# Gate and up products of a 4-bit-format feed-forward in three passes, and its rounding spread over two engines

## What is computed

```python
x = x + 0.5 * _L0_ffn_ref(_layernorm(x), w_gate, w_up, w_down)
x = x + _L0_attn_ref(_layernorm(x), L0_attn_W, L0_attn_b)
x = x + 0.5 * _L0_ffn_ref(_layernorm(x), w_gate, w_up, w_down)
x = x + 0.5 * _L1_ffn_ref(...)   # mixture of experts
x = x + _L1_attn_ref(...)        # causal attention
x = x + 0.5 * _L1_ffn_ref(...)
...
def fp4_quant_dequant(x):        # blocks of 16 along the last dim
    scale = max(max(abs(xb)) / 6.0, 1e-12)
    xn = xb / scale
    idx = searchsorted(_MID, abs(xn))        # grid 0, 0.5, 1, 1.5, 2, 3, 4, 6
    return _GRID[idx] * sign(xn) * scale
def fp4_linear(x, w):
    return einsum('bsk,nk->bsn', fp4_quant_dequant(x), fp4_quant_dequant(w))
gate, y = fp4_linear(x, w_gate), fp4_linear(x, w_up)     # 256 -> 704
h = silu(gate) * y
return fp4_linear(h, w_down)                              # 704 -> 256
```

## Time and profile before

| | us |
|---|---|
| median of three runs | 2346.11 (2342.72 to 2347.78) |
| span of the profiled execution | 2324.6 |
| first feed-forward, first to last L523 | 68.17 to 361.06 |
| second feed-forward, first to last L523 | 473.99 to 770.69 |
| TensorE busy in the span | 1960.7 (84%) |
| VectorE busy | 1764.5 (76%) |
| ScalarE busy | 958.9 (41%) |
| GpSimd busy | 907.5 (39%) |

### The profile page before, as it was taken

How to read it: one execution, slowest core, us unless ns; L and a number is a source line. 1 busy time by engine, 2 the same in 40 slices (tenths; PEclk the granted TensorE clock), 3 DMA queues, 4 the chain that set the end, 5 groups by cost and what they waited for, 6 DMA issues and landing times. The chain is left out here.

```text
span 2324.6 us, 36254 instructions
## 1 busy us (share of the span) xinstructions
PE 1960.7 (84%) x11363; PEld 1301.0 (56%) x11363; DVE 1764.5 (76%) x3598; ACT 958.9 (41%) x1892; POOL 907.5 (39%) x910
## 2 busy tenths in 40 slices
PE   2899997889999747989978599999999995398998
PEld 1566665756666426877866233333333363287787
DVE  7798874578887667877978577777777646687788
ACT  1222223322222443433557255555555537143345
POOL 2444442134444467887245300000000026588853
PEclk9999997989999858999989699999999996599999
DMA  5000000100000342223526534334334006222246
GB/s 177 1 0 0 0 0 14 42 0 1 0 0 0 97 159 64 92 87 101 170 69 168 98 55 70 51 54 69 50 55 70 2 1 195 75 89 89 89 148 191
DMA packets 116655, 156.59 MB, mean 67 GB/s; under 512 B 20966, under 2 KB 85772, under 8 KB 115980
## 3 DMA queue, kind: packets, MB, share of 16 engines
q1 hardware_dynamic: 99840, 112.83, 20.9%
q0 software_dynamic: 14400, 40.41, 5.6%
q10 hardware_dynamic: 2252, 1.29, 0.2%
HBM read 107.00 MB, written 47.20 MB: 66 GB/s over the span
## 5 line engine op out<-in xcount | busy, mean ns | idle before, releaser
L2021 DVE TENSOR_REDUCE t_nm<-ps 128x1 f32<-128x512 f32 (+3 forms) x768 | 390.9, 553 | 106.3 <-PE ps L2111 53.5
L2087 ACT ACTIVATE t_E<-ps 128x1024 f32<-128x1024 f32 (+3 forms) x384 | 295.0, 808 | 248.0 <-PE ps L2139 194.9
L1507 PE MATMUL ps<-m_w,m_xT 128*128 (+1 forms) x1248 | 347.1, 414 | 0.8 <-DVE m_xT L1587 0.8
L1507 PEld LDWEIGHTS ps<-m_w,m_xT 128*128 128x128 f32 x1248 | 222.5, 191 | 38.2 <-issue 1.4
L567 POOL TENSOR_TENSOR f_h<-f_h,f_hmagic 128x704 f32<-128x704 f32 x64 | 108.1, 1689 | 293.4 <-DVE f_h L209 293.4
L605 PE MATMUL ps<-wgT,f_xT 128*128 128x352 f32 x512 | 187.8, 516 | 38.5 <-DVE f_h L523 36.4
L2006 POOL COPY t_Va<-t_V 128x128 f32<-128x128 f32 x64 | 16.1, 295 | 491.7 <-DVE t_mp L2032 491.5
L2136 PE MATMUL ps<-t_Qs,t_Ks 98*128 98x512 bf16 (+3 forms) x768 | 199.8, 341 | 6.0 <-DMA t_Qs<-t_mT 4.1
L1525 PE MATMUL ps<-m_w,m_hT 128*128 (+1 forms) x1248 | 199.7, 296 | 0.5 <-DVE m_hT L1604 0.5
L639 PE MATMUL ps<-wdT,f_hT 128*128 128x256 f32 (+1 forms) x768 | 189.5, 389 | 7.4 <-DVE X L557 5.4
L1559 ACT ACTIVATE m_hT<-ps 128x256 fp32r<-128x256 f32 x208 | 80.1, 385 | 227.9 <-PE ps L1516 226.7
(11 more groups left out here) (296 smaller groups left out, 3950.0 us busy)
## 6 DMA issues: line engine op xcount, KB each, us to landing
m_raw<-in_L_ffn_rw SPq DMA_DIRECT2D x48, 256.0 KB, 3.3
t_parts<-t_qkv_part SPq DMA_DIRECT2D x64, 192.0 KB, 2.8
t_Qs<-t_parts SPq DMA_DIRECT2D x96, 128.0 KB, 4.0
t_Ks<-t_parts SPq DMA_DIRECT2D x96, 128.0 KB, 6.6
m_yl<-m_picked_out SPq DMA_DIRECT2D x40, 256.0 KB, 3.2
m_rows<-m_xn SPq DMA_DIRECT2D x16, 512.0 KB, 4.3
m_xg<-m_rows SPq DMA_DIRECT2D x64, 128.0 KB, 2.8
m_y<-m_picked_out SPq DMA_DIRECT2D x24, 256.0 KB, 3.3
```

The costliest lines, as they stand in the source:

```text
L1507: last = nc.tensor.matmul(ps[:, H1 + u, :], xT[:, u, kx, k, :], of_expert(w1, kw, e, k), start=n == 0, stop=n == 3 * DC - 1)
L2021: nc.vector.tensor_reduce(dst, ps[:, bank, 0:n], AX_X, ALU.max, negate=True).then_inc(emptied, 1)
L2087: nc.scalar.activation(E[:, s % NPB, :, 0:n], ps[:, bank:bank + 2, 0:n], ACT.Exp, scale=float(HD) ** -0.5).then_inc(e_ok, 1)
```

## The change

Four things are changed, all in the small-format feed-forwards.

1. `xT`, `wgT` and `wuT` become pairs of `fp32r` numbers, a high part (ScalarE's copy rounds it to the format) and a low part, which VectorE makes as PSUM value minus high part (`x_low` for the rows, `low` in `prepare` for the weights). `gate_up` issues three passes (high x high, high x low, low x high) per chunk and half, 24 matmuls a tile instead of 8 in fp32.
2. The rounding grid comes from ScalarE (`fp4_grid`: absolute value times a constant), and VectorE rounds in two operations (`fp4_snap`: max with a floor and add, then max with the floor and subtract). The three operations of `fp4_round_up` and GpSimd's subtraction go for `h`, the four operations of `fp4_round` for the rows. The weights keep `fp4_round`.
3. Because the snap waits for ScalarE, `make_h` ends with the division, and `snap_h(n + 1)` opens the next step; `h_finish` on GpSimd comes one step later as well. ScalarE's `h_make_grid(n + 1)` opens its step, ahead of the copies of the transposed `h`.
4. The row work moves: statistics from `j == 2` to `j == 1`, scales from 3 to 2, rounding from `j == 0` of the next group's turn to `j == 3`. The two row pieces are turned at `j == 0` and `j == 1`, each ahead of the down product. The factor `TIE` of the rows' scales goes from VectorE to GpSimd.

```diff
+GRID, FLOOR = RND - 2.0, 1.5 * RND
+PASSES = ((0, 0), (0, 1), (1, 0))
...
-        self.wgT = self.sb("wgT", [P, DC, FF4], ctx=self.until_fp4_done)
+        self.wgT = self.sb("wgT", [P, 2, DC, FF4], F32R, ctx=self.until_fp4_done)
...
+def fp4_grid(nc, a, grid):
+    return nc.scalar.activation(grid, a, ACT.Abs, scale=GRID)
+
+def fp4_snap(nc, a, grid):
+    nc.vector.scalar_tensor_tensor(out=a, in0=grid, scalar=FLOOR, in1=a, op0=ALU.max, op1=ALU.add)
+    nc.vector.drain()
+    return nc.vector.scalar_tensor_tensor(out=a, in0=grid, scalar=FLOOR, in1=a, op0=ALU.max, op1=ALU.subtract,
+                                          reverse1=True)
...
     def divide(self, pool, g):
         pool.wait_ge(self.scaled, g + 1)
+        pool.sem_inc(self.ch.fence, 1)
+        self.ch.nc.gpsimd.tensor_scalar(self.xs[:, 2, :], self.xs[:, 2, :], TIE, None, ALU.mult)
+        self.ch.nc.gpsimd.drain()
         fp4_times(self.ch.nc.gpsimd, self.flat, XB, self.xs[:, 2, :]).then_inc(self.divided, 1)
+    def grid(self, act, g):
+        act.wait_ge(self.divided, g + 1)
+        fp4_grid(self.ch.nc, self.flat, self.magic[:, :]).then_inc(self.gridded, 1)
     def rounding(self, dve, g):
-        dve.wait_ge(self.divided, g + 1)
-        fp4_round(self.ch.nc, self.flat, self.magic[:, :]).then_inc(self.rounded, 1)
+        dve.wait_ge(self.gridded, g + 1)
+        fp4_snap(self.ch.nc, self.flat, self.magic[:, :]).then_inc(self.rounded, 1)
...
+            def low(m):
+                wT = (ch.wgT, ch.wuT)[m]
+                dve.wait_ge(stored, m + 1)
+                for c in range(DC):
+                    b = 4 * m + 2 * c
+                    nc.vector.tensor_tensor(wT[:, 1, c, 0:512], ch.ps[:, b, :], wT[:, 0, c, 0:512], ALU.subtract)
+                    last = nc.vector.tensor_tensor(wT[:, 1, c, 512:FF4], ch.ps[:, b + 1, 0:FF4 - 512],
+                                                   wT[:, 0, c, 512:FF4], ALU.subtract)
+                last.then_inc(split, 1)
...
             scale_down(2)
+            low(0)
             rows.rounding(dve, 0)
             round_up_again(2)
+            low(1)
...
+            rows.grid(act, 0)
             act.wait_ge(turned, 3)
...
+            def x_low(g, c, par):
+                dve.wait_ge(x_high, 2 * g + c + 1)
+                nc.vector.tensor_tensor(xT[:, par, 1, c, :], ps[:, XTURN, :], xT[:, par, 0, c, :], ALU.subtract
+                                        ).then_inc(x_split, 1)
...
             def step(n, g, s, end):
-                j = s % GT
-                if j == 0 and has(g, 1):
-                    rows.rounding(dve, g + 1)
+                j, par = s % GT, (s // GT + 1) % 2
+                if exists(n, 1):
+                    snap_h(n + 1, (s + 1) % 4)
+                if j == 1 and has(g, 2):
+                    rows.stats(dve, g + 2)
                 if j == 2 and has(g, 2):
-                    rows.stats(dve, g + 2)
-                if j == 3 and has(g, 2):
                     rows.scales(dve, g + 2)
                 if exists(n, 2):
-                    make_h(n + 2, (s + 2) % 4)
+                    if j < DC and not end:
+                        make_h(n + 2, (s + 2) % 4, g + 1, j, par)
+                    else:
+                        make_h(n + 2, (s + 2) % 4)
+                if j == 3 and has(g, 2):
+                    rows.rounding(dve, g + 2)
...
             def h_finish(n, buf):
                 pool.wait_ge(h_round, n + 1)
-                nc.gpsimd.tensor_tensor(h[:, buf, :], h[:, buf, :], hmagic[:, buf % 2, :], ALU.subtract)
-                nc.gpsimd.drain()
                 fp4_times(nc.gpsimd, h[:, buf, :], HB, hs[:, buf, 1, :]).then_inc(h_quant, 1)
...
-                        for c in range(DC):
+                        for k, (c, (kx, kw)) in enumerate((c, m) for c in range(DC) for m in PASSES):
...
@@ TensorE, step @@
-                if j == 1 and not end:
-                    pe.wait_ge(rows.quantised, g + 2)
-                    x_turn(g + 1, 0)
+                if j < DC and not end:
+                    if j == 0:
+                        pe.wait_ge(rows.quantised, g + 2)
+                    pe.wait_ge(x_split, 2 * g + j + 2)
+                    x_turn(g + 1, j)
...
-                if j == 1 and not end:
-                    pe.wait_ge(x_stored, 2 * g + 3)
-                    x_turn(g + 1, 1)
...
@@ ScalarE, step @@
+                if exists(n, 1):
+                    h_make_grid(n + 1, (s + 1) % 4)
                 act.wait_ge(h_turned, n + 2)
...
+                if j == 3 and has(g, 2):
+                    rows.grid(act, g + 2)
...
@@ local_attention, ScalarE @@
+                    if k == 8:
+                        next_rows.grid(act, 0)
```

More of the change, by code:

```diff
@@ L229, in __init__ @@
         self.flat = self.xn[:, :, :].rearrange("p t d -> p (t d)")
-        (self.stats_ok, self.rstd_ok, self.xn_ok, self.scaled, self.divided, self.rounded, self.quantised) = (
-            ch.sem("fp4_" + k) for k in ("stats", "rstd", "xn", "x_scaled", "x_div", "x_round", "x_quant"))
+        (self.stats_ok, self.rstd_ok, self.xn_ok, self.scaled, self.divided, self.gridded, self.rounded,
+         self.quantised) = (ch.sem("fp4_" + k) for k in (
+             "stats", "rstd", "xn", "x_scaled", "x_div", "x_grid", "x_round", "x_quant"))
     def stats(self, dve, g):
@@ L255, in scales @@
         dve.wait_ge(self.xn_ok, g + 1)
-        fp4_scale(self.ch.nc, self.flat, XB, self.xs[:, 0, :], self.xs[:, 1, :], self.xs[:, 2, :]
+        fp4_scale(self.ch.nc, self.flat, XB, self.xs[:, 0, :], self.xs[:, 1, :], self.xs[:, 2, :], tie=False
                   ).then_inc(self.scaled, 1)
@@ L288, in prepare @@
         turned = ch.sem("w_turned")
-        stored = ch.sem("w_stored")
+        stored, split = ch.sem("w_stored"), ch.sem("w_low")
         mats = [(gate, FC * D), (up, FC * D), (down, DC * FF4)]
@@ L423, in _ @@
             pe.wait_ge(quant, 3)
-            pe.wait_ge(stored, 1)
+            pe.wait_ge(split, 1)
             for c in range(DC):
@@ L461, in _ @@
                     b = 4 * m + 2 * c
[L462 to L463 removed]
+                    nc.scalar.activation(wT[:, 0, c, 0:512], ch.ps[:, b, :], ACT.Copy)
+                    last = nc.scalar.activation(wT[:, 0, c, 512:FF4], ch.ps[:, b + 1, 0:FF4 - 512], ACT.Copy)
                 last.then_inc(stored, 1)
+            rows.grid(act, 0)
             act.wait_ge(turned, 3)
@@ L538, in _ @@
                 dve.wait_ge(ch.loaded_x, 16 * BATCHES)
+            for c in range(DC):
+                x_low(0, c, 0)
             rows.stats(dve, 1)
-            make_h(0, 0, True)
+            make_h(0, 0)
             rows.scales(dve, 1)
-            make_h(1, 1, True)
+            snap_h(0, 0)
+            make_h(1, 1)
+            rows.rounding(dve, 1)
             def step(n, g, s, end):
-                j = s % GT
-                if j == 0 and has(g, 1):
-                    rows.rounding(dve, g + 1)
+                j, par = s % GT, (s // GT + 1) % 2
[3 more added lines that the diff above has]
+                    rows.stats(dve, g + 2)
                 if j == 2 and has(g, 2):
-                    rows.stats(dve, g + 2)
-                if j == 3 and has(g, 2):
                     rows.scales(dve, g + 2)
                 if exists(n, 2):
-                    make_h(n + 2, (s + 2) % 4)
+                    if j < DC and not end:
[4 more added lines that the diff above has]
+                    rows.rounding(dve, g + 2)
                 if not first and isinstance(n, int) and n == TILES - 2:
@@ L566, in h_finish @@
                 pool.wait_ge(h_round, n + 1)
-                nc.gpsimd.tensor_tensor(h[:, buf, :], h[:, buf, :], hmagic[:, buf % 2, :], ALU.subtract)
-                nc.gpsimd.drain()
                 fp4_times(nc.gpsimd, h[:, buf, :], HB, hs[:, buf, 1, :]).then_inc(h_quant, 1)
             rows.rstd(pool, 1)
+            rows.divide(pool, 1)
             h_finish(0, 0)
-            rows.divide(pool, 1)
-            h_finish(1, 1)
+            rows.rescale(pool, 1)
             def step(n, g, s, end):
                 j = s % GT
-                if j == 0 and has(g, 1):
-                    rows.rescale(pool, g + 1)
+                if exists(n, 1):
+                    h_finish(n + 1, (s + 1) % 4)
+                if j == 1 and has(g, 2):
+                    rows.rstd(pool, g + 2)
                 if j == 2 and has(g, 2):
-                    rows.rstd(pool, g + 2)
+                    rows.divide(pool, g + 2)
                 if j == 3 and has(g, 2):
-                    rows.divide(pool, g + 2)
-                if exists(n, 2):
-                    h_finish(n + 2, (s + 2) % 4)
+                    rows.rescale(pool, g + 2)
             turns(pool, step)
@@ L663, in _ @@
                 act.wait_ge(ch.loaded_x, 16 * BATCHES)
-            x_store(0, 0, 0)
-            x_store(0, 1, 0)
+            for c in range(DC):
+                x_hi(0, c, 0)
             silu(0)
             x_normalise(1)
```

(13 more changed lines are left out.)

42 lines of the change are left out of this document (22 added, 20 removed).

## The result

| | before | after |
|---|---|---|
| median of the runs, same chip | 2344.41 us (2342.00 to 2347.78) | 2278.66 us (2275.94 to 2280.99) |
| ratio after to before | | 0.9701 [0.9666, 0.9736] |
| span of the profiled execution | 2324.6 us | 2275.9 us |

What follows compares the result with a forecast made beforehand. VectorE was taken to bound the feed-forwards in four-tile groups; each falls to 265.2 us, saving 27.7 and 31.5, less +2.2 start-up: -57 us from 2346.1 gives 2289, range 2258 to 2318.

Steps and rivals of the forecast that it cites:

- What bounds: In the feed-forwards before the change, VectorE sets the pace in groups of four tiles, TensorE 3.5 us a group behind.
- VectorE's group of 34.7: Four feed-forward tiles on VectorE: 30.75 us of work, 1.7 grid waits, 1.7 GpSimd hold, 0.6 short operations beside GpSimd.
- TensorE's pass: One of 24 gate and up passes a tile takes 0.175 us, so 4.2 us a tile instead of 4.74.
- The sum: One feed-forward: opening 17.5, six groups 208.2, last five intervals 39.5, together 265.2 us against 292.9 and 296.7.
- Start-up +1.1: Ahead of each feed-forward's first tile, pieces pass ScalarE and VectorE before the next turn: +1.1 us, twice.
- Tail nothing: After the last tile the chain loses a GpSimd operation and gains a grid; taken as nothing.
- The median against the span: For the whole kernel, the median's 21.5 us above the profiled span of 2324.6 lies around the span and stays.
- B: Rival at the group's first snap: GpSimd's lock doesn't reach this operation, 24 us less, 2265; chance 0.15.
- C: Rival on TensorE: short waits lower its granted clock once a group, +1.4 us x 12, 2306; chance 0.12.
- D: Rival in gate and up: passes cost as much as 512-column ones, 5.9 us a tile, 2366; chance 0.05.
- E: Rival on ScalarE: the grid comes 0.8 us later in each tile, 3.2 us x 12, 2327; chance 0.08.
- The doubt written last: The four-tile period might be set by a hidden TensorE wait, for h_stored behind the grid or the second low part.

Runs made afterwards that it cites:

- gps_reads_twice: The changed kernel with one more GpSimd operation reading the rows and scales into a spare buffer ahead of the rows' rescale; 2334.69 us.
- stats_behind_snap: The changed kernel with the next row group's statistics moved behind the rows' snap, where GpSimd rescales; 2275.63 us, ratio 0.9694 to the kernel before.
- part 1 undone: The changed kernel with gate and up back in fp32 matmuls, 8 a tile, without low parts; 2293.36 us, ratio 0.974 to the kernel before.
- after_again: The changed kernel run once more, unedited; 2285.14 us, ratio 0.9710 to the kernel before.
- before_again: The kernel before, unedited, profiled once more in one execution; 2365.07 us, span 2363.3.
- gps_writes_first: The changed kernel with a GpSimd fill of 2048 columns, which reads nothing, ahead of the rows' rescale; 2315.69 us.
- low_after_div: The changed kernel with the rows' low part made behind the division of h instead of behind the product; 2283.45 us, ratio 0.9730 to the kernel before.
- rounding_undone: The changed kernel with VectorE making the rounding constant again, GpSimd subtracting it from h, and no ScalarE grid; 2347.78 us, ratio 0.9977 to the kernel before.
- moves_alone: The changed kernel with three-pass products and new rounding both undone, only the row work's moved steps kept; 2365.40 us, ratio 1.0048 to the kernel before.

## Why the prediction was right, step by step

- **What bounds**: right. VectorE sets the group's period: in the changed kernel its only idle time in a group is the three grid waits, a longer hold lengthens the period (gps_reads_twice) and without the hold it is shorter (stats_behind_snap). TensorE needs 30.7 us with the passes; with part 1 undone it is full at 34.2, only 0.3 under VectorE's period. One sign just missed: TensorE was to be under 93% busy and shows 213.10 of 229 us, 93.1%.
- **VectorE's group of 34.7**: 34.5. The hold by GpSimd's rescale was put at 1.7 and is 1.62; the grid wait at 0.57 and is 0.53, three times; the short operations beside GpSimd at 0.6 and are 0.71; the statistics' operation on four columns fell from 1.13 to 0.17, as foreseen.
- **TensorE's pass**: mis-sized. Put at 0.175 from the line between 256 and 512 columns, it is 0.164; a tile is 7.44, not 7.8, and the last five intervals 36.75, not 39.5. That is 5.5 us of the error, all at the ends, as the step said: 3.6 by the tile (2 x 5 x 0.36, of it 2.6 by the pass), 1.9 because the remainder of 0.5 wasn't needed and the first of the five intervals was shorter than a tile. The formula of the Trainium skill, TensorE: Matmul & The Clock Gate, "Back-to-back issue gap", gives 0.149 as an estimate; the page has it for a single matmul by itself and says that a stream of weight loads and matmuls departs from it, which the prediction left out. The measured pass lies between the two.
- **The sum**: 265.2 a feed-forward, measured 261.8 and 261.7; 6.9 us less in all, by the last five intervals 5.5, by the groups 1.8, by the openings 0.4 more. The groups came out 0.4% under their sum and the ends 7% under theirs; the total is close because the ends are the short stretch.
- **Start-up +1.1**: 69.26 - 68.17 = 1.09 in the first; that the figure fits so well is luck, for in after_again the first product starts at 71.40. Ahead of the second it failed: from the last residual addition to the first product it is 95.29 us instead of 98.75. The stage between holds waits and clock levels of its own; which of them gave the difference stays open. From the start to the last product the two traces differ by 67.8 us (770.69 - 702.91), before_again and after_again by 72.3, both near the 65.7 of the medians.
- **Tail nothing**: 14.90 us from the last product to the last addition, 14.18 before; the down product of 4.74 us behind a wait of 1.71 [the row at 336.31] against 3.02 in before.
- **The median against the span**: failed. The prediction took the 21.5 us between median and span as lying around the span. Around it lie 1.8 us (the profiled execution of the changed kernel took 2277.73, its span 2275.9); the rest is that the profiled execution of before was a short one behind the feed-forwards (1554 us, 1588 in before_again). It did no harm, because the sum was subtracted from the median.
- **Rivals**: B (no hold) fell with the 2.51 us; gps_reads_twice and gps_writes_first show what holds the snap. C (the clock) didn't come: after a wait of 1.42 us the next records take what they take without one (2.95 for twelve of down), and the clock is 1.00; it came where an edit lengthened the waits. D (dear passes) fell with 0.164. E (a late grid) fell with 0.53. The doubt written last, a wait for the second low part, isn't there in the changed kernel; low_after_div shows it 2.00 us long when that part is made later.
- **What was weighed wrongly**: the rule of the Trainium skill, SBUF — State Buffer, "Who interferes with whom", was read as speaking against the change, since two-input steps replace one-input ones. In the runs one-input operations of the old rounding are held as well (1.97 for 0.53), and between rounding_undone and the changed kernel, where GpSimd's subtraction goes too, the hold falls from 4.3 to 2.3 us a group.

## What to carry to other kernels

Sum each engine's starts over the loop's own period, with the time one engine holds another and the hand-offs included: here the total came out within half a per cent. Where a hold or a wait was left out of the same kind of sum, it missed by 3.0 us of 37.8 a group (rounding_undone) and by 2 to 3 of 39 (moves_alone). Give each part of a change its own sum, for a part that is a loss alone (the passes, 3%) can be a small gain behind another. A step moved to hide one wait is worth only what the next resource on that path lets through: here 0.9 of 1.6 us, then a wait for ScalarE. Where single executions differ by 35 us in stages that nobody touched, compare the touched stages in the traces and the medians on one chip.
